# One-hots of the gathered edges on ScalarE, their ends prepared in the message stage, keys by halves, the last two steps written out, in a graph network on one core

## The reference

```python
h = relu(layernorm(x))
m = relu(concat(h[src], edge_attr) @ w1a + b1a) @ w1b + b1b       # per edge, 96 wide
agg = segment_sum(m, dst) / max(count, 1)
x = x + relu(concat(h, agg) @ w2a + b2a) @ w2b + b2b
h = relu(layernorm(x))
f = h
for _ in range(10):                                                # propagation
    f = segment_sum((f * src_norm)[src], dst) * dst_norm
    f = 0.9 * f + 0.1 * h
x = x + f
```

## Time and profile before

| | us |
|---|---|
| median of 3 runs | 6043.35 |
| lowest and highest | 6040.39, 6046.41 |
| the profiled execution, its own time | 6041.42 |
| its span, first to last instruction | 6039.8 |
| busy in the span: PE, VectorE, ScalarE, POOL | 4938.6, 4018.9, 789.6, 4296.1 |
| instructions in the span | 196,769 |

### The profile page before, as it was taken

How to read it: one execution, slowest core, us unless ns; L and a number is a source line. 1 busy time by engine, 2 the same in 40 slices (tenths; PEclk the granted TensorE clock), 3 DMA queues, 4 the chain that set the end, 5 groups by cost and what they waited for, 6 DMA issues and landing times. The chain is left out here.

```text
span 6039.8 us, 196769 instructions
## 1 busy us (share of the span) xinstructions
PE 4938.6 (82%) x76542; PEld 3090.9 (51%) x76542; DVE 4018.9 (67%) x11958; ACT 789.6 (13%) x1725; POOL 4296.1 (71%) x4300
## 2 busy tenths in 40 slices
PE   1675555555555553999999999999999999999997
PEld 1565455555555542555555555555555555555554
DVE  7897766777776777666566666656666666665655
ACT  0343333333333310000000000000000000000000
POOL 5777777777777764775767767676776767767675
PEclk9987777777777776999999999999999999999998
DMA  4543333333333312656556555555555556555655
GB/s 126 130 122 99 97 95 101 95 96 95 101 97 99 92 56 88 211 198 217 194 208 214 198 207 200 209 202 209 205 202 212 201 207 211 198 209 198 219 198 178
DMA packets 530050, 980.42 MB, mean 162 GB/s; under 512 B 295962, under 2 KB 461306, under 8 KB 483146
## 3 DMA queue, kind: packets, MB, share of 16 engines
q1 hardware_dynamic: 377002, 841.91, 39.8%
q0 software_dynamic: 136864, 97.04, 7.8%
q10 hardware_dynamic: 15232, 28.37, 1.3%
HBM read 775.11 MB, written 204.68 MB: 162 GB/s over the span
## 5 line engine op out<-in xcount | busy, mean ns | idle before, releaser
L1798 POOL DMA_INDIRECT x_nodes_fast<-feature_rows,x_nodes_fast x2560 | 2591.6, 1012 | 1050.6 <-issue 853.3
L2103 PE MATMUL banks_fast<-count_units_fast,feature_parts_fast 128*32 128x512 fp8e3 x58848 | 3230.6, 380 | 50.1 <-DVE gathered_hots L1983 34.4
L2103 PEld LDWEIGHTS banks_fast<-count_units_fast,feature_parts_fast 128*32 128x32 bf16 x58848 | 1586.8, 97 | 1592.7 <-issue 64.8
L1917 DVE TENSOR_SCALAR count_units_fast<-packed_ring_fast 128x512 int32<-128x512 int32 x2459 | 1063.8, 433 | 1332.7 <-PE banks_fast L2103 1291.2
L146 POOL DMA_INDIRECT rows_fast<-row_table,idx_fast x1456 | 1418.6, 974 | 443.7 <-issue 405.6
L1918 DVE TENSOR_SCALAR count_units_fast<-packed_ring_fast 128x512 int32<-128x512 int32 x2459 | 1055.8, 429 | 0.0
L1225 DVE TENSOR_SCALAR window_place_hot_fast<-iota_wide_fast,local_keys_fast,target_weight_fast 128x196 bf16<-128x196 f16 x3136 | 951.0, 349 | 0.0
L1335 PE MATMUL banks_fast<-identity_fast,rows_fast 128*128 128x128 f32 x784 | 221.2, 375 | 671.8 <-DMA rows_fast<-row_table,idx_fast 671.8
L1318 PE MATMUL banks_fast<-window_place_hot_fast,window_src_hot_fast 128*128 128x196 bf16 x3136 | 611.5, 282 | 21.9 <-DVE window_place_hot_fast L1225 14.8
L1324 PE MATMUL banks_fast<-window_place_hot_fast,window_src_hot_fast 128*128 128x196 bf16 x3136 | 596.3, 277 | 0.0
L1335 PEld LDWEIGHTS banks_fast<-identity_fast,rows_fast 128*128 128x128 f32 x784 | 97.8, 174 | 724.5 <-DMA rows_fast<-row_table,idx_fast 592.1
(11 more groups left out here) (315 smaller groups left out, 2187.4 us busy)
## 6 DMA issues: line engine op xcount, KB each, us to landing
packed_ring_fast<-edge_counts SPq DMA_DIRECT2D x352, 1792.0 KB
edge_counts<-count_stage_fast SPq DMA_DIRECT2D x100, 784.0 KB, 3.9
running_sums<-run_sums_fast SPq DMA_DIRECT2D x100, 768.0 KB, 3.6
x_nodes_fast<-feature_rows,x_nodes_fast POOLq DMA_INDIRECT x2560
rows_fast<-row_table,idx_fast POOLq DMA_INDIRECT x1456
feature_rows<-feature_parts_fast ACTq DMA_DIRECT2D x50, 384.0 KB
rows_fast<-attrs_padded SPq DMA_DIRECT2D x98, 128.0 KB
attrs_padded<-in_edge_attr SPq DMA_DIRECT2D x1, 12500.0 KB, 42.3
```

What stands on the lines that cost most here:

```text
L1798: pool.indirect_dma_start(out=rows[:, g % GSLOTS, i, :], out_offset=None, in_=b.dram.feature_rows[side], in_offset=bass.IndirectOffsetOnAx ...
L1917: nc.vector.tensor_scalar(to[..., 0:P // 8], of, NIBBLES, None, ALU.bitwise_and)
L2103: last = nc.tensor.matmul(b.banks[at:at + DN, SWEEP[half_of(side, m)], 0:COLS], parts[:, side, j, k * DN:(k + 1) * DN], of_strip.bitcast(FP8),
```

## The change

Four things change.

1. Keys by halves: a key fetch brings 128 rows, the keys of two pairs, one in each half of the partitions. There are 4 fetches a loop (behind pairs 1, 3, 5 and 6) instead of 7; `turn_keys` picks the half by a half of the identity.
2. The ends of the last 32,768 edges are loaded, worked out, transposed and copied at the start of the message stage, and the checks of bounds are made there. Row numbers (`gather_idx`) and negated places (`minus_local`) have memory of their own; `hots` shares memory with the ring of gathered rows, and several tiles of the node network move into tiles of the edges.
3. ScalarE makes the one-hots in the node network: for each of 256 columns the square of (column number less place), and for four columns together a rectifier of (1 less square). Of 64 such pieces 16 come before the loop over g and 8 ahead of everything else at each even g from 4 to 14. VectorE's one-hots and checks in the propagation go, and so do the waits for them.
4. The propagation's loops on VectorE, PE, ScalarE and SP run 4 times, and the last two steps are written out behind them. The last step loads and opens nothing for a next one, makes the result itself (three operations instead of eight, the last adds x, loaded into `parts[:, 0]` ahead of chunk 2 of that step) and stores it block by block from ScalarE's queue. `store_result` is left out of the fast way; `needs_general` waits for the stores.

The core of the diff:

```diff
+KEY_FETCHES = (AHEAD_GROUPS + 1) // 2
...
+        fetch_behind = {pair: pair // 2 for pair in (*range(1, AHEAD_GROUPS, 2), AHEAD_GROUPS - 1)}
...
+            nc.gpsimd.iota(first_i, pattern=[[P * P // PER_TARGET, 2]],
+                           base=N - P * FIRST_GATHERED - P // 2 - (GATHERS * P - P // 2) // PER_TARGET,
+                           channel_multiplier=P // PER_TARGET).then_inc(bounds_made, 1)
...
+                if t % SLOTS and t // SLOTS in fetch_behind:
+                    r_keys = fetch_behind[t // SLOTS]
+                    pool.wait_ge(keys_pointed, i * KEY_FETCHES + (r_keys + 2))
                     pool.sem_inc(taken, 1)
-                    fetch_keys((t // SLOTS + KEYS_AHEAD) % AHEAD_GROUPS)
...
+            make(nc.vector.tensor_copy(first_f, first_i))
+            make(nc.vector.tensor_scalar(first_f, first_f, 0.0, float(TILES * P - P), ALU.max, ALU.min))
+            make(nc.vector.tensor_scalar(first_f, first_f, float(P * FIRST_GATHERED), None, ALU.add))
+            dve.wait_ge(ends_in, 32)
+            make(nc.vector.tensor_scalar(low_i, src_i, P - 1, None, ALU.bitwise_and))
+            make(nc.vector.tensor_scalar(high_i, src_i, BITS, None, ALU.logical_shift_right))
+            make(nc.vector.tensor_copy(src_low, low_i))
+            make(nc.vector.tensor_copy(src_high, high_i))
+            make(nc.vector.scalar_tensor_tensor(out=src_row, in0=src_low, scalar=float(J), in1=src_high, op0=ALU.mult, op1=ALU.add))
+            make(nc.vector.tensor_copy(dst_f, dst_i))
+            for h in range(2):
+                make(nc.vector.tensor_scalar(local_f[:, h * P:(h + 1) * P], dst_f[:, h * P:(h + 1) * P], first_f[:, h:h + 1], None, ALU.subtract))
+            make(nc.vector.tensor_scalar(outside, local_f, 0.0, None, ALU.is_lt))
+            make(nc.vector.tensor_scalar(beyond, dst_f, float(P * FIRST_GATHERED), None, ALU.is_ge))
+            make(nc.vector.tensor_tensor(outside, outside, beyond, ALU.mult))
+            make(nc.vector.tensor_reduce(bad[:, 0:1], outside, AX.X, ALU.max))
+            make(nc.vector.tensor_tensor(bad[0:1, 0:1], bad[0:1, 0:1], beyond[0:1, 0:1], ALU.max))
+            make(nc.vector.tensor_scalar(outside, local_f, float(P), None, ALU.is_ge))
+            make(nc.vector.tensor_reduce(bad[:, 1:2], outside, AX.X, ALU.max))
+            make(nc.vector.tensor_tensor(bad[:, 0:1], bad[:, 0:1], bad[:, 1:2], ALU.max))
+            make(nc.vector.tensor_tensor(unsorted[:, :], unsorted[:, :], bad[:, 0:1], ALU.max))
...
+            for ends, to in ((ins["src"], src_i), (ins["dst"], dst_i)):
+                act.dma_start(to.rearrange("p (h e) -> p h e", h=2),
+                              ends[E - GATHERED_EDGES:E].rearrange("(h c e) -> c h e", h=2, e=P)).then_inc(ends_in, 16)
+            act.wait_ge(ends_turned, 1)
+            nc.scalar.copy(gather_idx[:, :], b.banks[:, C_BANK[3], 0:GATHERS]).then_inc(ends_kept, 1)
+            nc.scalar.mul(minus_local[:, :], b.banks[:, C_BANK[3], GATHERS:2 * GATHERS], -1.0).then_inc(ends_kept, 1)
...
+                                            b.ident[:, half * LW:(half + 1) * LW], start=True, stop=True, skip_group_check=True)
...
+            pe.wait_ge(ends_made, 3 + 8)
+            for of, what in enumerate((src_row, local_f)):
+                for h in range(2):
+                    at = of * GATHERS + h * P
+                    last = nc.tensor.transpose(b.banks[:, C_BANK[3], at:at + P], what[:, h * P:(h + 1) * P], b.ident[:, :])
+            last.then_inc(ends_turned, 1)
...
+            PIECES, EARLY_PIECES, PIECES_A_GAP = GATHERS // PIECE, 16, 8
+
+            def keep_hots(n):
+
+                act.wait_ge(squared, (n + 1) * PIECE)
+                nc.scalar.activation(hots[:, n * PIECE:(n + 1) * PIECE, :], off_target[:, n % 2, :, :], ACT.Relu,
+                                     scale=-1.0, bias=1.0).then_inc(hots_made, 1)
+
+            def make_hots(n):
+
+                if n >= 2:
+                    act.wait_ge(hots_made, n - 1)
+                for c in range(n * PIECE, (n + 1) * PIECE):
+                    nc.scalar.activation(off_target[:, n % 2, c % PIECE, :], b.iota[:, :], ACT.Square,
+                                         bias=minus_local[:, c:c + 1]).then_inc(squared, 1)
+                if n:
+                    keep_hots(n - 1)
+                if n == PIECES - 1:
+                    keep_hots(n)
+
+            for n in range(EARLY_PIECES):
+                make_hots(n)
             for g in range(GROUPS + SKEW):
+                if g % 2 == 0 and g >= 2 * SKEW:
+                    first = EARLY_PIECES + (g - 2 * SKEW) // 2 * PIECES_A_GAP
+                    for n in range(first, min(first + PIECES_A_GAP, PIECES)):
+                        make_hots(n)
                 if g >= SKEW and (g - SKEW) % 2:
...
+            def load_two_steps(tt):
+
                 for g in range(2 * STEP_CHUNKS):
-                    m, k = divmod(g % STEP_CHUNKS, CHUNKS)
+                    side, c = divmod(g, STEP_CHUNKS)
+                    m, k = divmod(c, CHUNKS)
+                    if finishes(tt, side) and c == RING:
+                        sp.wait_ge(unit_used, UNITS + (STEPS - 1) * STEP_UNITS)
+                        sp.wait_ge(head_swept, STEPS - 1)
+                        sp.wait_ge(table_stored[0], 16 + (PAIRS - 1) * STORES * 16)
+                        sp.dma_start(x_again, b.dram.x_saved).then_inc(x_returned, 16)
 
                     sp.wait_ge(opened, tt * (2 * STEP_UNITS) + (g + 1) * UNITS)
                     sp.sem_inc(passed, 1)
                     load(g % RING, k, m)
 
-            for c in range(RING):
-                sp.wait_ge(opened, STEPS * STEP_UNITS + (c + 1) * UNITS)
-                load(c, c, 0)
-            sp.wait_ge(group_used, GSLOTS + (STEPS - 1) * STEP_GROUPS + (J * DN * 4 // P) // GROUP + 1)
-            sp.dma_start(x_back(hots), b.dram.x_saved).then_inc(x_returned, 16)
-            for slot in range(RING):
...
-            pool.wait_ge(idx_made, 1)
-            with pool.Fori(0, steps2) as tt:
+            pool.wait_ge(x_kept, 16)
+            with pool.Fori(0, PAIRS) as tt:
...
+            def store_result(where):
+
+                whole = min(where.stop, J - 1)
+                act.dma_start(out[P * where.start:P * whole, :].rearrange("(j p) d -> p j d", p=P),
+                              per_node(b.f[:, :])[:, where.start:whole, :]).then_inc(result_stored, 16)
+                if whole < where.stop:
+                    act.dma_start(out[P * whole:N, :], b.f[0:NL, whole * DN:(whole + 1) * DN]).then_inc(result_stored, 16)
...
+            def result(q, got, taken, done, where):
+
+                tiles = where.stop - where.start
+                t1 = per_node(scaled[:, 0:tiles * DN])
+                f, h, x = (per_node(of)[:, where, :] for of in (b.f[:, :], b.h[:, :], x_again))
+                nc.vector.tensor_tensor(t1, per_node(got), gain[:, where].unsqueeze(2).broadcast_to([P, tiles, DN]), ALU.mult).then_inc(result_made, 1)
+                dve.wait_ge(result_made, q * 3 + 1)
+                dve.sem_inc(taken, 1)
+                nc.vector.scalar_tensor_tensor(out=f, in0=h, scalar=ALPHA, in1=t1, op0=ALU.mult, op1=ALU.add).then_inc(result_made, 1)
+                dve.wait_ge(result_made, q * 3 + 2)
+                dve.wait_ge(x_returned, 16)
+                nc.vector.tensor_tensor(f, f, x, ALU.add).then_inc(result_made, 1)
+                dve.wait_ge(result_made, q * 3 + 3)
+                dve.sem_inc(done, 1)
+
             def new_features(q, side, got, taken, done, where):
...
             early = UNITS + AHEAD
-            for v in range(UNITS):
+            for v in range(early):
                 open_unit(0, 0, v)
-            PIECE = 32
-            for c in range(0, GATHERS, PIECE):
-                nc.vector.tensor_tensor(hots[:, c:c + PIECE, :], b.iota16[:, :].unsqueeze(1).broadcast_to([P, PIECE, P]),
-                                        local16[:, c:c + PIECE].unsqueeze(2).broadcast_to([P, PIECE, P]), ALU.is_equal).then_inc(hots_made, 1)
...
-            dve.wait_ge(hots_made, GATHERS // PIECE)
-            with dve.Fori(0, steps2) as tt:
+
+            def two_steps(tt):
...
+                            elif not finishes(tt, side):
                                 open_unit(tt + 1, 0, v - STEP_UNITS)
...
-            pe.wait_ge(hots_made, GATHERS // 32)
-            with nc.Fori(0, steps2, engines=[pe.engine], hint_back_edge=True) as tt:
...
+                            if not finishes(tt, side):
+                                sweep_units(t + 1, 0, 1 - side, 0, AHEAD)
...
+            sp.wait_ge(result_stored, RESULT_STORES * 16)
...
+            with nc.Fori(0, PAIRS - 1, engines=[pe.engine], hint_back_edge=True) as tt:
+                two_steps(tt)
+            two_steps(PAIRS - 1)
```

231 lines of the change are left out of this document (111 added, 120 removed).

## The result

The changed kernel takes 5950.1 us (median of 4 runs, 5947.9 to 5957.2) beside 6043.4 for the kernel before: a ratio of 0.9848, with a 95% interval of 0.9831 to 0.9865. The forecast was 5958.5 and its range 5946 to 5983. The profiled execution spans 5949.2 us where the one before spanned 6039.8, and the 90.6 us between them divide by stages as follows. The limits of a stage are one event in both traces: POOL's first iota of the message stage, ScalarE's first copy of the node network, the issue of the head's load, the first and the last of ScalarE's 50 drains.

What follows compares the result with a forecast made beforehand. PE was taken to bound the propagation and POOL the message stage. Terms -25.7 + 0 + 6.2 - 40.3 + 0 - 25.0 = -84.8 us gave 5956.6 profiled, 5958.5 us as median, range 5946 to 5983.

Steps and rivals of the forecast that it cites:

- Part 1, keys: Message stage, POOL: 29 key fetches of 128 rows at 1.28 us replace 51 costing 62.7 us; -25.7 us (-27 to 0).
- Part 2, ends: Start of the message stage: preparing ends delays PE's first turn of keys by 16 us, covered by 46; 0 us (0 to +10).
- Part 3, one-hots on ScalarE: Node network: 64 pieces of 1.84 us mostly fill ScalarE's idle gaps, the last root comes 5.6 late; +6.2 us (+2 to +32).
- the rival of a second table set: Node network: squares need another table than roots, adding reloads of 18 us, 5972; part of ScalarE being too slow, chance 0.14.
- nothing is covered beyond the gap: Node network: PE's last multiplication and VectorE stand behind a late rectifier; about 0.2 us missed in each of two gaps.
- Part 4, start: Start of the propagation: PE reaches unit 2 at 2368.5 instead of 2407.84, without waiting for one-hots; -40.3 us (-44 to -32).
- PE starts at 2364: Start of the propagation: first chunk lands at 2363, a middle between 2357.5 and 2367.90, and PE starts 1.0 us behind.
- the 0.5 for a late POOL and the 0.5 for the second chunk: Start of the propagation: +0.5 us for POOL's gathers 5.7 us behind unit 2, and +0.5 for the second chunk's landing.
- The second start at a low clock: Start of the propagation: PE's second slow start, 62 ns a matmul against 57, goes away; -2.0 us.
- Part 5, straight code: Propagation: three loop passes and two steps written out change PE's issue waits little; 0 us (-1.4 to +3).
- Part 6, end: End of the kernel: shorter sweep and last features, no addition, a 256 KB last store; -25.0 us (-27 to -19).
- The slower rival: Last two steps: straight code starves PE, 1.4 us per instruction piece, slower from 61 stalls, 6079 at all 86; chance 0.03.

Runs made afterwards that it cites:

- Part 1 alone: The kernel before with the key fetches by halves and nothing else of the change: 6018.2 us, ratio 0.9943 to the kernel before.
- the changed kernel again: The changed kernel run once more, unedited, on the chip of the last experiments: 5958.4 us beside 6050.1 for the kernel before, ratio 0.9846.

## Why the prediction was right, and where it was not

The profiled execution gained 5.8 us more than the sum. The message stage gave 6.7 more than its term, the ten steps 2.0 and the node network 0.9, the start 3.9 less than its term. That these partly cancel is luck; the execution shown had the shortest message stage of eleven.

**Part 1, keys (-25.7).** Right: the fetches' rows give back 62.9 - 37.2 = 25.7 us. The stage's -32.4 contains 5.5 us of row gathers that were quicker in that execution and about 1 us of other wander; over eleven executions the stage is on average 27.8 us shorter than the one of before.

**Part 2, ends (0).** Right. Part 1 alone and the changed kernel again, which differ by it in this stage, took 1984.31 and 1984.57 us; as the stage wanders by 8 us, the timeline of the kernel after says more. PE turns the ends (L1364) and then still waits for the first keys (L1352):

```profile
178.33 1.12 PE L1364 MATMUL banks_fast<-identity_fast,f_nodes_fast 128*128 128x128 f32 x4 [19.86 <-DVE f_nodes_fast L1231]
...
182.09 1.08 PE L1352 MATMUL banks_fast<-identity_fast,raw_keys_fast 128*128 128x64 f32 x4 [2.64 <-DMA raw_keys_fast<-edge_keys,key_idx_fast]
```

The first turn of keys comes at 182.09 instead of 181.62, so the 46 us of cover that the forecast counted were hardly used; no wait of POOL ahead of a gather or a fetch of that stage is longer than 0.3 us.

**Part 3, one-hots on ScalarE (+6.2).** The size came out, +5.3, with the piece at 1.83 for 1.84 and the last root 5.22 late for 5.6. This term does not hang on the wander of the stage: in every kernel with eight pieces in a gap and the rest at the end the last root came 15.79 us after the one before it, and 10.57 in every other. ACT_TABLE_LOAD appears once in the run, 1.283 us as in the earlier trace rows, so the rival of a second table set fell. The Trainium skill, page "ScalarE: Activation LUTs", section "What ACT_TABLE_LOAD costs", gives the price of such operations: 280 ns and 0.833 ns a column with a pointer as bias, 93 ns of overlap, 186 ns without the pointer. Worked out from these figures of the Trainium skill, the estimate for a piece is 4 x 0.294 + 0.613 = 1.79 us and for a single square 0.387; the trace agrees, with 1.83 and 0.390 measured. One sentence of the step failed: "nothing is covered beyond the gap". VectorE's 3.04 us were a wait for the group before, and in the row looked at a rectifier could be some 3.5 us late. It did no harm to the sum, since the gaps were missed by 0.2 us only, but by it nine pieces in a gap, which clear the end, were priced at a loss.

**Part 4, start (-40.3, measured -36.4).** The mechanism was right: the one-hots were the wait that ended last, as the experiment with them on VectorE shows, and PE goes through without a second start. The size was 3.9 us short. Mis-sized was the term "PE starts at 2364", 16.2 us after the head's issue: it was 21.3. The forecast took the head's landing, 9.7 us, from the earlier trace rows, where the stores were issued behind the loads of the ends; with those gone the stores begin 1.1 us earlier, x is saved after 7.7 us instead of 14.4, and the head needs 16.0. That the stores are what delays it is shown by the experiment that holds them back (6.5 us); that 1.1 us make this much of a difference is the likely reading, and was not run by itself. The forecast removed something from a queue without asking what moves up in it. Against that, the feature rows landed 5.5 us earlier, POOL was level with PE, and the 0.5 for a late POOL and the 0.5 for the second chunk were not needed. The second start at a low clock, -2.0 in the forecast, is gone as it said: the windows of after show one, and those of before showed two, 0.63 from 2368 to 2374 and 0.60 from 2407 to 2415.

**Part 5, straight code (0).** Right: the ten steps differ by 2.0 us, and the last two are as long as the others: from first drain to first drain the steps alternate between 356.6 to 357.6 and 361.6 to 362.0 us, the last of these (step 9 to 10) with 356.58; and the last step took 291.5 us from its first drain to its last, the other even steps 291.3 to 291.7. PE's waits for issue went from 5.6 us at four places and 1.1 at two of the head's sweep to 6.8 and 2.6, and fully written out they were 7.8. The ten steps wander by 10 us, so the 0 is shown to that, and by these waits. The Trainium skill, page "Runtime: NRT & Kernel Launch", section "Instruction fetch mechanics", says that branches break the sequential prefetch and that kernels prefer unrolling where possible. The trace agrees that a branch costs something: in the kernel after PE waits 1.0 to 1.8 us at the three back edges and 2.3 at the way out of the loop. A gain from unrolling all of it is not seen here. That x comes back in the last step costs nothing that the rows show.

**Part 6, end (-25.0).** Right to 0.1 us, in its steps too: VectorE's last features begin 1.00 us after the last drain instead of 3.51, so 2.5 earlier, as forecast. Counted from the last drain they end at 4.45 us (4.35 forecast), the flags at 8.3 (8.35) and the span at 13.74 (13.75). The last store, 256 KB instead of the whole result, carries 10.9 of it.

The slower rival did not come: the 61 stalls of 1.4 us that it needs are not there even with all ten steps written out, where PE waits for issue nine times, 7.8 us in all.

## What to carry to other kernels

An idle engine can be cheaper than a fast one: ScalarE needs over three times VectorE's time for these one-hots, but as most of that lies in gaps in which nobody waits for it, it cost 5 us and gave 36. When an operation is taken out of a queue, ask what moves up behind it and whose bandwidth that takes; bytes that left the start altogether gave 10 us where reordering them gave 3. To say that a row's wait is for the instruction just edited, look for that instruction's own successor by its start time: the same line of the group before may be what it waits for.

## What was not expected of the hardware

An indirect DMA costs POOL nearly the same for 64 rows (0.930 us) and for 128 (0.978), and 0.30 us of issue in either case.

Beside VectorE's 4.4 us operations with two inputs POOL's gathers took 4.03 us each in the kernel with one-hots on VectorE, eight of eight, where they take 0.96 alone; in the kernel before a single one took 34.23 us beside all eight. What makes the difference between these two is open. Two inputs are not the whole of it: in the kernel with the head's load on ScalarE's queue the first gather took 3.58 us beside VectorE's operations of 0.42 us with one input.

The head's load of 1568 KB landed in 6.5 to 6.8 us with no large stores beside it, in 9.7 where 3920 KB of stores were issued from another queue 1.1 us after it, and in 16.0 where they were issued with it. In the two kernels that reorder the loads the granted clock was full (2.4 GHz) before PE's wait of 3.9 and 5.0 us for gathered rows, and 0.57 and 0.68 on average in the stretch of 8 us in which PE went on.
